# Attention contexts kept with features on partitions: two heads add up in the same rows, and row sums come from ScalarE and VectorE

## The reference

```python
x = emb[inp]                                   # (64, 128, 256)
q, k, v = x @ Wq.T + bq, x @ Wk.T + bk, x @ Wv.T + bv       # 16 heads of 16 features
scores = einsum('bhqd,bhkd->bhqk', q, k) / sqrt(16)
ctx = einsum('bhqk,bhkd->bhqd', softmax(scores), v)
h = ctx @ Wo.T + bo
xn = layernorm(h)
h = h + sigmoid(xn @ gate_w.T + gate_b) * exclusive_scan(decay, (xn @ B_w.T) @ C_w.T)
h = h + layernorm(h) @ sign(weight).T
```

## Time and profile before

| | |
|---|---|
| median of 3 runs | 752.07 us (751.53 to 752.09) |
| profiled execution | 753.01 us |
| its span in the trace | 751.3 us |
| granted TensorE clock, mean | 0.971 |
| busy: PE, ACT, DVE, POOL | 694.7, 580.5, 516.6, 377.1 us |

### The profile page before, as it was taken

How to read it: one execution, slowest core, us unless ns; L and a number is a source line. 1 busy time by engine, 2 the same in 40 slices (tenths; PEclk the granted TensorE clock), 3 DMA queues, 4 the chain that set the end, 5 groups by cost and what they waited for, 6 DMA issues and landing times. The chain is left out here.

```text
span 751.3 us, 21201 instructions
## 1 busy us (share of the span) xinstructions
PE 694.7 (92%) x7047; PEld 650.4 (87%) x7047; DVE 516.6 (69%) x1147; ACT 580.5 (77%) x1643; POOL 377.1 (50%) x431
## 2 busy tenths in 40 slices
PE   4589999999999999999999999999999999999862
PEld 3478999999999999999999999999999999998762
DVE  3556677777877777677777777777767777786532
ACT  2588988888888888888888888888888888888410
POOL 7402355555545654556445545465455555544443
PEclk9799999999999999999999999999999999999875
DMA  5323233333222333332223333332223333321000
GB/s 142 113 86 102 83 115 113 100 113 112 89 75 83 104 112 102 107 112 97 71 85 96 112 111 99 112 103 69 87 91 112 112 98 112 109 81 37 16 15 28
DMA packets 56016, 69.68 MB, mean 93 GB/s; under 512 B 6768, under 2 KB 41648, under 8 KB 55984
## 3 DMA queue, kind: packets, MB, share of 16 engines
q1 hardware_dynamic: 52048, 60.48, 24.1%
q0 software_dynamic: 3072, 8.39, 5.3%
q10 hardware_dynamic: 864, 0.40, 0.2%
HBM read 10.52 MB, written 8.39 MB: 25 GB/s over the span
## 5 line engine op out<-in xcount | busy, mean ns | idle before, releaser
L372 ACT ACTIVATE probs<-ps_s,neg_max 128x128 f32<-128x128 f32 x1024 | 295.5, 383 | 75.2 <-DVE neg_max L518 75.2
L518 DVE TENSOR_REDUCE neg_max<-ps_s 128x4 f32<-128x512 f32 x256 | 175.6, 686 | 111.5 <-PE ps_s L641 110.0
L381 ACT COPY probsT<-ps_t 128x512 f32<-128x512 f32 x256 | 155.4, 607 | 17.6 <-PE ps_t L717 11.6
L294 POOL TENSOR_TENSOR xn<-h,mv 128x512 f32<-128x512 f32 x64 | 66.6, 1041 | 197.6 <-DVE ve L545 197.6
L717 PE MATMUL ps_t<-ident,probs 128*128 128x128 f32 x1024 | 153.9, 273 | 6.5 <-ACT probsT L381 6.2
L717 PEld LDWEIGHTS ps_t<-ident,probs 128*128 128x128 f32 x1024 | 119.5, 141 | 13.0 <-issue 5.2
L641 PE MATMUL ps_s<-k_stack,q_stack 128*128 128x256 f32 x512 | 123.8, 323 | 4.0 <-DMA q_stack<-q_low 4.0
L307 POOL TENSOR_TENSOR state_high<-state_in,ones_col 128x512 fp32r<-128x512 f32 x32 | 33.2, 1037 | 112.4 <-DVE state_in L630 112.4
L641 PEld LDWEIGHTS ps_s<-k_stack,q_stack 128*128 128x128 f32 x512 | 77.6, 192 | 4.4 <-DMA q_stack<-q_low 4.4
L287 POOL DMA_INDIRECT x_emb<-in_emb,id_col x64 | 65.1, 1018 | 23.2 <-issue 14.2
L533 DVE BATCH_NORM_STATS2 stats<-h 128x6 f32<-128x256 f32 x128 | 48.2, 418 | 33.9 <-POOL h L319 32.8
(11 more groups left out here) (126 smaller groups left out, 1893.8 us busy)
## 6 DMA issues: line engine op xcount, KB each, us to landing
k_stack<-k_high SPq DMA_DIRECT2D x128, 128.0 KB
q_stack<-q_high SPq DMA_DIRECT2D x64, 256.0 KB
k_stack<-k_low SPq DMA_DIRECT2D x64, 128.0 KB
q_stack<-q_low SPq DMA_DIRECT2D x32, 256.0 KB
out<-y SPq DMA_DIRECT2D x32, 256.0 KB, 2.1
x_emb<-in_emb,id_col POOLq DMA_INDIRECT x64, 3.8
raw<-in_wkT SPq DMA_DIRECT2D x1, 256.0 KB, 3.1
raw<-in_wqT SPq DMA_DIRECT2D x1, 256.0 KB, 4.1
```

What stands on the lines that cost most here:

```text
L294: nc.gpsimd.tensor_tensor(xn[:], h[:], mv[:, :, 0:1].to_broadcast([P, 2, D]), ALU.subtract).then_inc(centred, 1)
L372: last = nc.scalar.activation(probs[s % 2][:, j], ps_s[s % 2][:, j * SEQ:j * SEQ + SEQ], ACT.Exp, bias=neg_max[s % 2][:, j:j + 1])
L381: nc.scalar.copy(probsT[st][:], ps_t[:]).then_inc(act_pT, 1)
L518: nc.vector.tensor_reduce(neg_max[s % 2][:], ps_s[s % 2][:].rearrange("p (h k) -> p h k", h=HPS), axis=AX.X, op=ALU.max, negate=True).then ...
```

## The change

The context stays with features on partitions and is never turned. v_wide holds, for two halves a of the 16 heads, rows of 16 zero columns and then per head 16 columns of v and 16 of zero. A 32-column window that starts at v of head i of the first half puts its context into the first 16 rows of a group of 32; a window that starts 16 columns earlier puts head i of the second half into the last 16 rows. Both add up in the same 32 rows of ps_c (first matmul of the pair of heads with start, second with stop), so ps_c holds both sequences of a pair in one bank. The rows of woT are reordered on the host to fit.

The row sums no longer come from a column of ones. For steps 0 to 3 ACT's exponentials give them (accum_out); for steps 4 to 7 DVE adds up probs (sums). ACT waits before it overwrites probs that DVE still reads. DVE takes one reciprocal of all 32 sums (invert_sums, behind the first moments), POOL spreads each over 16 columns (inv_wide, ahead of its first normalise), PE turns these to features (invert_rows, after step 3), ACT copies them (move_inverse), and DVE multiplies ps_c by them (normalise_context, where the second context_norm stood). ACT takes the high part of the product (move_ctx), POOL the low part (behind h), and the projection with wo follows as before. DVE's ctxTl goes. PE's matmuls with wk now come after the inverses' transposes, and their bank's wait changes. probsT is freed once a sequence and no longer once a step. bv is loaded twice, side by side, and the memsets of ones go.

```diff
 # POOL, after state_low
+                if exists(t - 1):
+                    await_event(pool, dve_inv, 1, t - 1, 1)
+                    await_event(pool, pe_inv, 1, t - 2, 1)
+                    nc.gpsimd.tensor_tensor(
+                        inv_wide[:], inv_sum[:].rearrange("p b i a -> p (b i a)").unsqueeze(2).to_broadcast([P, 2 * HEADS, HD]),
+                        ones_col[:, 0:1].unsqueeze(1).to_broadcast([P, 2 * HEADS, HD]), ALU.mult).then_inc(pool_inv, 1)
                 if exists(t - 2):
                     await_event(pool, dve_ve1, 1, t - 2, 1)
                     normalise(t - 2, t - 3, h0[par], mv1, ve1, rs1, xn1, pe_xn1T, centred1, rs1_done, pool_xn1)
...
                     nc.gpsimd.tensor_tensor(h1[:], gated[:], h0[1 - par][:], ALU.add).then_inc(pool_h1, 1)
+                if exists(t - 1):
+                    await_event(pool, act_ctxT, 1, t - 1, 1)
+                    await_event(pool, pe_o, 1, t - 2, 1)
+                    nc.gpsimd.tensor_tensor(ctxT[1][:], ctx_feat[:], ctxT[0][:].bitcast(fp32),
+                                            ALU.subtract).then_inc(pool_ctxlo, 1)
 # ACT
+                        if s >= 6:
+                            await_event(act, dve_sum, 4, t, s - 5)
+                        elif s < 2:
+                            await_event(act, dve_sum, 4, t - 1, s + 3)
                         for j in range(HPS):
+                            taken = row_sum[par][:, 0, s * HPS + j:s * HPS + j + 1] if s < 4 else None
                             last = nc.scalar.activation(probs[s % 2][:, j], ps_s[s % 2][:, j * SEQ:j * SEQ + SEQ],
-                                                        ACT.Exp, bias=neg_max[s % 2][:, j:j + 1])
+                                                        ACT.Exp, bias=neg_max[s % 2][:, j:j + 1], accum_out=taken)
...
                 move_probsT(2)
-                move_ctx(t - 1, 1)
                 exponentials(2)
                 move_probsT(3)
+                move_inverse(t - 1)
                 exponentials(3)
...
                 move_probsT(4)
+                move_ctx(t - 1)
                 exponentials(4)
...
                 move_probsT(6)
-                move_block(t - 1, ctxT[0], g2, pe_ctxT, pe_o, act_ctxT)
-                move_ctx(t, 0)
                 exponentials(6)
 # DVE
+                def sums(s):
+                    pair, st = before(t, s, 1)
+                    if exists(pair):
+                        await_event(dve, act_exp, STEPS, pair, st + 1)
+                        nc.vector.tensor_reduce(row_sum[par if s else 1 - par][:, 1, st % 4 * HPS:st % 4 * HPS + HPS], probs[st % 2][:],
+                                                axis=AX.X, op=ALU.add).then_inc(dve_sum, 1)
+                def invert_sums():
+                    if exists(t - 1):
+                        await_event(dve, act_exp, STEPS, t - 1, 4)
+                        await_event(dve, dve_sum, 4, t - 1, 4)
+                        await_event(dve, pool_inv, 1, t - 2, 1)
+                        nc.vector.reciprocal(inv_sum[:].rearrange("p b i a -> p b a i"),
+                                             row_sum[1 - par][:].rearrange("p b (a i) -> p b a i", a=2)).then_inc(dve_inv, 1)
+                def normalise_context():
+                    if exists(t - 1):
+                        await_event(dve, pe_pv, 2, t - 1, 2)
+                        await_event(dve, act_inv, 1, t - 1, 1)
+                        await_event(dve, pool_ctxlo, 1, t - 2, 1)
+                        nc.vector.tensor_tensor(ctx_feat[:].rearrange("p c b s -> p (c b s)"), ps_c[:], inv_rows[:],
                                                 ALU.mult).then_inc(dve_ctx, 1)
...
                 maxima(0)
+                sums(0)
...
                     norm_moments(stats1, mv1, ve1, dve_mv1, dve_ve1, t - 2)
-                context_norm(0, g1)
+                invert_sums()
...
-                context_norm(1, g2)
+                normalise_context()
...
                 maxima(5)
+                sums(5)
...
                 maxima(6)
-                low_features(t - 1, ctxT, g2, act_ctxT, pe_o, dve_ctxlo)
+                sums(6)
                 maxima(7)
+                sums(7)
 # PE
+                    for c in range(C):
+                        at = slice((2 * c + b) * SEQ, (2 * c + b + 1) * SEQ)
+                        for a in range(2):
+                            for j in range(4):
+                                i = 4 * c + j
+                                head = HALF * a + i
+                                values = v_wide[vp][:, b, a, HD - HD * a + VW * i:HD - HD * a + VW * i + VW]
+                                last = mm(ps_c[VW * j:VW * j + VW, at], values,
+                                          probsT[head // HPS + 4 * b][:, head % HPS], a == 0, a == 1)
+                    last.then_inc(pe_pv, 1)
+                def invert_rows(dst):
+                    await_event(pe, pool_inv, 1, t - 1, 1)
...
-                if exists(t - 1):
-                    await_first((act_tanh, 1, t - 3, 1), (dve_klo, C, t, C))
-                    context_rows(0, g1)
...
                 attention(3)
+                if exists(t - 1):
+                    await_first((dve_v, 1, t, 1), (dve_h0, 1, t - 2, 1))
+                    invert_rows(g2)
...
-                    await_first((dve_v, 1, t, 1), (dve_h0, 1, t - 2, 1))
-                    context_rows(1, g2)
...
-                    await_event(pe, dve_ctx, 2, t - 1, 2)
-                    to_features(g2, lambda b: ctx_tok[:, b], pe_ctxT)
```

More of the change, by code:

```diff
@@ L107, in build @@
         probsT = [sb(f"probsT{p}", [P, HPS, SEQ]) for p in range(8)]
-        ctx_raw = [sb(f"ctx_raw{b}", [P, 4, SEQ]) for b in range(2)]
-        inv_sum = sb("inv_sum", [P, 2, HEADS])
-        ctx_tok = sb("ctx_tok", [P, 2, D])
+        inv_sum, inv_wide = sb("inv_sum", [P, 2, HALF, 2]), sb("inv_wide", [P, 2 * HEADS, HD])
+        inv_rows, ctx_feat = sb("inv_rows", [P, C * 2 * SEQ]), sb("ctx_feat", [P, C, 2, SEQ])
         h0 = [sb(f"h0{p}", [P, 2, D]) for p in range(2)]
@@ L379, in move_probsT, with move_inverse, move_ctx @@
                         await_event(act, pe_pT, STEPS, pair, st + 1)
-                        await_event(act, pe_pv, STEPS, pair - 1, st + 1)
+                        await_event(act, pe_pv, 2, pair - 1, st // 4 + 1)
                         nc.scalar.copy(probsT[st][:], ps_t[:]).then_inc(act_pT, 1)
-                def move_ctx(pair, b):
+                def move_inverse(pair):
                     if exists(pair):
-                        await_event(act, pe_pv, STEPS, pair, 4 * b + 4)
-                        await_event(act, pe_ctxrow, 2, pair - 1, b + 1)
-                        nc.scalar.copy(ctx_raw[b][:], ps_c[:]).then_inc(act_ctx, 1)
+                        await_event(act, pe_inv, 1, pair, 1)
+                        await_event(act, dve_ctx, 1, pair - 1, 1)
+                        nc.scalar.copy(inv_rows[:], g2[:]).then_inc(act_inv, 1)
+                def move_ctx(pair):
+                    if exists(pair):
+                        await_event(act, dve_ctx, 1, pair, 1)
+                        await_event(act, pe_o, 1, pair - 1, 1)
+                        nc.scalar.copy(ctxT[0][:], ctx_feat[:]).then_inc(act_ctxT, 1)
                 def move_block(pair, dst, src, filled, freed, done):
@@ L720, in context @@
                 def context(s):
-                    for back in (6, 5, 4, 3):
-                        pair, st = before(t, s, back)
-                        if not exists(pair):
-                            continue
-                        vp = par if s >= back else 1 - par
-                        b, g = divmod(st, 4)
-                        await_event(pe, act_pT, STEPS, pair, st + 1)
-                        if st == 0:
-                            await_event(pe, dve_v, 1, pair, 1)
-                            await_event(pe, act_ctx, 2, pair - 1, 2)
-                        if st == 4:
-                            await_event(pe, act_ctx, 2, pair, 1)
-                        for j in range(HPS):
-                            last = mm(ps_c[VW * j:VW * j + VW, g * SEQ:g * SEQ + SEQ],
-                                      v_aug[vp][:, b, g * HPS + j], probsT[st][:, j])
-                        last.then_inc(pe_pv, 1)
@@ L739, in context_rows @@
-                def context_rows(b, dst):
-                    await_event(pe, act_ctx, 2, t - 1, b + 1)
-                    for g in range(4):
-                        last = nc.tensor.transpose(dst[:, g * P:g * P + P], ctx_raw[b][:, g], ident[:])
-                    last.then_inc(pe_ctxrow, 1)
+                    pair, st = before(t, s, 3)
+                    if not exists(pair):
+                        return
+                    vp = par if s >= 3 else 1 - par
+                    b = st // 4
@@ new lines, in context @@
+                    last.then_inc(pe_pv, 1)
+                def invert_rows(dst):
```

(9 more changed lines are left out.)

64 lines of the change are left out of this document (32 added, 32 removed).

## The result

The changed kernel takes 834.5 us (median of 4 runs, 833.32 to 835.08) against 751.8 (751.34 to 752.09): ratio 1.110, 95% interval 1.108 to 1.112, so +82.7 us where +40 was forecast. The profiled execution took 835.08 us, its span is 833.3. The direction and the place were right, the size was half.

The account below looks back on a forecast made before the run. PE bound the kernel at 21.1 us a turn, a 20.6 us loop through DVE and POOL just behind. Adding 1.14 + 1.21 - 0.04 gave 22.9: +1.5 over 28 turns, -2 at the ends, 792 us; range 766 to 836 (0.85).

Parts of the forecast that it names:

- a: ACT, exponentials of steps 0 to 3: extra time for each row sum, taken as 0.1 us, estimated 0.09 from the skill.
- ctxTl called hidden: POOL's low part of the context, behind h: 1.28 us, hidden before the next state_in; at most 1.3 without that cover.
- the reciprocal is on it: +0.21 behind ve: DVE, behind the first moments: the reciprocal now lies on POOL's path and adds 0.21 us a turn.
- against 0.59 of slack: POOL at h: reciprocal and inv_wide delay h by 0.21 + 1.0 us, of which the 0.59 wait for gated absorbs part.
- rival E: PE gets dearer: column groups' overlap lost (860 us) or clock falling to 0.83 with idle time (829 us); chance 0.03.
- The first three turns are PE's own and save up to 0.9 each: Start of the kernel: PE alone sets these turns and gains; with the end put at nothing, together -2 us.
- C: Part of the loop's growth is hidden in unseen idle time: turn 22.0 to 22.6, 766 to 783 us; chance 0.09.
- B: ACT binds on top of the loop if a exceeds 0.185: 814 us at 0.25, 841 at 0.33; chance 0.24.
- D: Faster: PE stays the bound, loop growth under about 0.5 us, PE's 0.88 a turn comes out: 726 us; chance 0.07.
- gain and growth cancel: Whole kernel: PE's saving and the loop's growth offset each other, 752 us; chance 0.03.
- A: The loop through DVE and POOL binds: turn 22.9 us, 792 us, from 783 to 799; chance 0.54.
- E = 1.76: ACT between step 1's exponentials and k_low: longest time for a step's four exponentials that still fits, in us.

Follow-up runs that it names:

- the two additions to the kernel before: Kernel before plus POOL's unused spread ahead of its first normalise: 779.9 us; kernel before plus DVE's four unused row sums: 774.1 us; both at once: 809.8 us.

## Why the prediction was right in its course and half in its size

**What bounds the kernel, and what would become late.** Right, but for the clock. The loop from wg to wg over step 7, state_in, step 0, y, step 1, POOL's normalise, h and xn1Tl sets the turn of the changed kernel, and every mark named for it is there but one, the unchanged clock: inv_wide directly behind the reciprocal, h free of gated, PE idle 2 us before wg, state_in at wg + 7.6 (399.17 - 391.59), row sums back to back with the maxima. That both parts cost, and share a part of the slack, is shown by the two additions to the kernel before.

**The terms of the sum.** Row sums: 0.60 each between starts against 0.57, the same 0.68 long as the maxima from PSUM. Of the shorter overhead on SBUF that the Trainium skill gives (Perfetto Trace Analysis, Optimizing Scalar/DVE Operations) nothing was seen. inv_wide 1.0: as forecast. PE's transposes and context matmuls: as forecast. a: four exponentials with sums take 401.16 to 402.55 = 1.39 us against 1.4, so 0.09 a sum; the read's own row is 0.237 us long on average, but most of it overlaps. The estimate of 0.09 that the prediction worked out from the Trainium skill (ScalarE: Activation LUTs, What ACT_TABLE_LOAD costs) was met.

**Where the size went wrong.** The forecast was +1.5 us a turn over 28 turns and -2 at the ends; measured were +2.58 over 27 and +12.5 at the ends. The steps that failed are the growth of POOL's path (1.21 against 0.59 of slack), ctxTl called hidden, the clock and the ends. Per turn the difference of 1.1 us has these terms:
- The step "the reciprocal is on it: +0.21 behind ve". It is 0.35 long at 32 columns, not 0.26 as at 16, and POOL started 0.61 behind ve's end (404.57 to 405.18) in one turn and 0.44 in the next, against 0.08 without it. So 0.4 to 0.5 instead of 0.21: +0.25.
- The step "against 0.59 of slack". Up to 0.25 of it was a gap behind id_col that stays: 0.15 on average over the two kinds of turn. It was readable: idle time before an instruction is slack only down to what the instruction needs after its own engine's last one.
- Contention: the second ve takes 0.45 instead of 0.17, since POOL's ctxTl, which I had called hidden, runs beside it: +0.28 with xn1Tl behind it. In time this couldn't be shown alone: in the run with the low part later it is gone, but as much came up at step 7's maxima.
- The wait between h's stats and the product, 0.98 to 1.05 against 0.94: +0.07.
- The clock, 0.30 to 0.39. I had it as rival E with 0.03, argued away by a stretch at 83% with clock 1.00. That stretch had no wait of 2 us ahead of wg; in the changed kernel the clock fell right behind such a wait, with PE busy for 20.8 us of a turn of 23.5.
- I compared with a turn of 21.44, a longer one; the mean is 21.33: 0.11.
- The two sums take 1.19 and not 1.14: +0.05. And the wait at step 0's maxima that they take the place of was worth 0.32 and not the 0.23 of idle time, since an instruction that has waited overlaps nothing: -0.09.

0.25 + 0.15 + 0.28 + 0.07 + 0.30 + 0.11 + 0.05 - 0.09 = 1.12, against the 1.08 found. The single terms come from one or two turns, so the last tenth isn't theirs to tell.

**The ends.** "The first three turns are PE's own and save up to 0.9 each" was wrong. Between DVE's first v and its fourth lie 60.2 us (34.59 to 94.83) against 55.0 (33.71 to 88.68): in the filling turns PE waits for exponentials and copies, and there ACT's sums and DVE's are in the way. At the end the turn before the last stores takes 24.2 us (757.02 to 781.24) against 19.7 (679.49 to 699.23), because the loop still binds where PE has little left to do. This is read from the traces; no run took it apart.

**The rivals.** The measured 834.5 lies inside 766 to 836, and near E's 829, by luck: the range was that wide for C, for B at the lower values of a, and for the lesser case of E. None of them is what happened, except that the clock fell, for 0.30 to 0.39 of the 2.58. D (faster) and "gain and growth cancel" did not come near. D's price of 0.88 a turn didn't fit the prediction's own sum either: even without any growth the loop's 20.6 stands above PE's 20.2. A's upper end of 799 is 797 by its own terms. B did not bind in the changed kernel, as forecast, but its limit of E = 1.76 was misplaced by 0.39/3 = 0.13, since k_low waits for both halves; that mistake cost nothing here and 12 us where the loop was short. E's first half, the loss of the column groups' overlap, was excluded by the block's unchanged 1.08 us.

## What to carry to other kernels

A change that takes work off the busiest engine must be priced on the loop that ends just behind it: a wait of 0.3 us that recurs in each turn names that loop, and what the change puts on it counts, less the slack, on however idle an engine. Slack belongs to a place: a wait takes up only what is added ahead of it on the engine that waits, and idle time ahead of an instruction can be a gap that stays. Put the new steps of a side path (here the inverses) where their engine is already waiting, and split a reduction over the idle stretches of two engines: the same idea then gave -2% instead of +11%. When a shorter loop brings no time, look at the granted clock before looking for another bound.

## What the runs showed of the hardware that I had not expected

- A wait of PE of about 2 us ahead of wg was followed in some turns by some 3 us at 1.2 GHz (wg's 14 matmuls in 3.15 us instead of 1.76). With the wait in each turn at 1.8 to 2.3 us, one turn in five was hit in the changed kernel, and most in the one with all sums from ACT. Ten extra matmuls in the wait ended it in both.
- A tensor_scalar of 128x2 on VectorE took 0.45 us instead of 0.17 while a 128x512 GpSimd instruction ran; a 128x512 reduction beside GpSimd stayed at 0.68.
- An exponential with an accumulator output is two instructions, 0.36 and 0.19 us or more long, and costs ScalarE 0.09 us between starts.
- A reciprocal of 32 columns took 0.35 us against 0.26 for 16.
